# Moving a 3 MB weight load behind ten gathers, and three row sums to other places in VectorE's order, in a transformer tower on one core

## What is computed

```
def _L0_ffn_ref(x, ...):                            # mixture
    shared_out = swiglu(x, shared_gate, shared_up, shared_down)
    top_id = argmax(x @ gate_w.T); score = sigmoid(max(x @ gate_w.T))
    routed_out = sum over e of swiglu(where(top_id == e, x * score, 0), r_gate[e], r_up[e], r_down[e])
    return shared_out + routed_out

h = h + _L0_ffn_ref(_layernorm(h), ...)
h = h + _L1_attn_ref(_layernorm(h), ...)            # first: s = max(abs(x)) / 127 over the whole array, round(x / s)
h = h + _L1_ffn_ref(_layernorm(h), qweights, scales, ...)   # w = (q / 7.5 - 1) * scale
```

## Time and profile before

| what | value |
|---|---|
| median of 3 timed runs | 531.59 us (531.07 to 534.79) |
| profiled execution, its own time | 535.75 us |
| its span, first to last instruction | 533.9 us |
| PE busy | 413.0 us (77% of the span) |
| DVE busy | 313.8 us (59%) |
| ACT busy | 243.6 us (46%) |
| POOL busy | 154.4 us (29%) |
| mean granted TensorE clock | 0.862 of full speed |

### The profile page before, as it was taken

How to read it: one execution, slowest core, us unless ns; L and a number is a source line. 1 busy time by engine, 2 the same in 40 slices (tenths; PEclk the granted TensorE clock), 3 DMA queues, 4 the chain that set the end, 5 groups by cost and what they waited for, 6 DMA issues and landing times.

```text
span 533.9 us, 9523 instructions
## 1 busy us (share of the span) xinstructions
PE 413.0 (77%) x3502; PEld 305.2 (57%) x3503; DVE 313.8 (59%) x846; ACT 243.6 (46%) x519; POOL 154.4 (29%) x192
## 2 busy tenths in 40 slices
PE   5788864687999999999889976631894247699997
PEld 4556632565788866666546774210442135589996
DVE  2989877898364212223212137669898987636643
ACT  4345552566554112222122113792397568566651
POOL 3488762899120700000000063017010001213310
PEclk9999986699798999999999997565556556999999
DMA  8941113950033240111110081000000000000002
GB/s 275 401 176 21 21 24 70 425 234 2 1 132 136 92 126 26 54 41 41 39 41 29 26 319 30 1 1 2 2 0 0 1 6 1 1 0 2 1 20 75
DMA packets 19793, 38.64 MB, mean 72 GB/s; under 512 B 2136, under 2 KB 16164, under 8 KB 18340
## 3 DMA queue, kind: packets, MB, share of 16 engines
q1 hardware_dynamic: 18788, 35.41, 19.2%
q0 software_dynamic: 960, 2.62, 1.4%
HBM read 29.77 MB, written 7.01 MB: 69 GB/s over the span
## 4 chain that ended last, share of the span: by engine, by line
PE 56%; DVE 22%; ACT 11%; issue 6%; POOL 3%; DMA 1%; DVEq 0%; SPq 0%; ACTq 0%; POOLq 0%
PE psum L1331 11%; PE psum L1338 6%; PE psum L1363 6%; PE psum L2423 4%; PE psum L1377 4%; PE psum L2456 3%; PE psum L890 2%; PE psum L2462 2%; PE psum L1002 2%; PE psum L1355 1%; ACT experts L1739 1%; PE psum L2440 1%; DVE tile_peak L1767 1%; DVE front L1766 1%; PE psum L641 1%
## 5 line engine op out<-in xcount | busy, mean ns | idle before, releaser
L1331 PE MATMUL psum<-experts,ring 128*128 x136 | 64.3, 596 | 1.9 <-issue 1.2
L1155 DVE TENSOR_TENSOR ring<-ring,psum 128x512 f32<-128x512 f32 x17 | 11.7, 688 | 62.9 <-PE psum L1331 62.9
L1262 POOL DMA_INDIRECT front<-expert_results,slot_of x10 | 9.8, 981 | 125.0 <-DMA expert_results<-ring 122.2
L1338 PE MATMUL psum<-front,shared 128*128 128x256 f32 (+1 forms) x160 | 36.0, 380 | 0.0
L1331 PEld LDWEIGHTS psum<-experts,ring 128*128 128x128 f32 x136 | 23.3, 190 | 19.5 <-issue 19.4
L1338 PEld LDWEIGHTS psum<-front,shared 128*128 128x128 f32 x160 | 30.3, 197 | 3.5
L1363 PE MATMUL psum<-experts,ring 128*128 x136 | 32.1, 379 | 0.0
L1363 PEld LDWEIGHTS psum<-experts,ring 128*128 128x128 f32 x136 | 25.8, 190 | 10.3 <-issue 7.6
L2423 PE MATMUL psum<-experts 128*128 128x256 f32 (+1 forms) x120 | 27.5, 372 | 4.6 <-ACT experts L2486 4.6
L1461 ACT COPY ring<-psum 128x512 f32<-128x512 f32 x17 | 10.0, 586 | 42.4 <-PE psum L1355 42.4
L641 PE MATMUL psum<-experts,ring 128*128 128x256 f32 x108 | 25.1, 382 | 3.5 <-DVE experts L500 1.5
(11 more groups left out here) (364 smaller groups left out, 1081.5 us busy)
## 6 DMA issues: line engine op xcount, KB each, us to landing
experts<-in_experts SPq DMA_DIRECT2D x8, 1536.0 KB, 12.1
experts<-in_x SPq DMA_DIRECT2D x9, 384.0 KB, 8.4
expert_rows<-zeros SPq DMA_DIRECT2D x1, 2176.0 KB, 14.7
ring<-expert_rows SPq DMA_DIRECT2D x17, 128.0 KB, 2.1
shared<-in_shared SPq DMA_DIRECT2D x1, 1536.0 KB, 18.2
experts<-in_ffn_q SPq DMA_DIRECT2D x1, 1536.0 KB
experts<-in_ffn_s SPq DMA_DIRECT2D x1, 1536.0 KB
experts<-in_pos_embed SPq DMA_DIRECT2D x1, 1152.0 KB, 9.3
```

Of the source, the lines that this page charges most:

```text
L1155: nc.vector.tensor_tensor(o, o, up_bank(g), ALU.mult).then_inc(hidden_done.sem, 1)
L1331: mm = nc.tensor.matmul(bank, sl_xT[t % 2][:, k, :], slot_w(t, block, k, F), start=(k == 0), stop=(k == KD - 1))
L1338: mm = nc.tensor.matmul(o[:, b, 0:w], shared_w(block, k, (2 * half + b) * P, P), moe_x(c)[:, k, 0:w], start=(k == 0), stop=(k == KD - 1))
```

## The change

Two edits. On SyncE, the two 1.5 MB loads now wait until all ten gathers have landed. On VectorE, `row_sums(0)` stands ahead of `shared_added(3)` instead of behind it, and `row_sums(3)` stands behind the row shifts of pairs 0 and 1 instead of ahead of them. No instruction is added or taken away other than the five waits on SyncE.

```
                 if g == GROUPS:
                     row_sums(dve, step, 2)
-                    row_sums(dve, step, 3)
                     row_shift(dve, 0)
                     row_shift(dve, 1)
+                    row_sums(dve, step, 3)
+                if g == GROUPS - 2:
+                    row_sums(dve, step, 0)
                 if g >= 1 and shared_step(g - 1) is not None and shared_step(g - 1)[1] == 1:
                     shared_added(shared_step(g - 1)[0])
                 if g == GROUPS - 2:
-                    row_sums(dve, step, 0)
                     row_sums(dve, step, 1)
...
             sp.wait_ge(sl_down.sem, sl_down.done(SLOT_TILES - 1))
+            for c in range(NCH):
+                sp.wait_ge(rows_back[c], 32)
             sp.dma_start(ffn_q, ins["ffn_q"]).then_inc(l_ffn.sem, 16)
             sp.dma_start(ffn_s, ins["ffn_s"]).then_inc(l_ffn.sem, 16)
```

## The result

The changed kernel has a median of 531.00 us against 533.43 us for the kernel before (18 runs each). The ratio is 0.9959, with a 95% interval of 0.9940 to 0.9978: faster by 2.2 us, and by 1.2 to 3.2 within the interval. The forecast was a gain of 2.4 and a median of 529.2; the gain came, and the median stands 1.8 higher because the kernel before has 533.43 over these 18 runs and not the 531.59 of its first three.

A forecast was written before the change was run, and what follows sets the result against it. TensorE was taken as late through gathers slowed by the loads and VectorE's order. The mark's 327.75 - 325.35 = 2.4 us gain gave 531.59 - 2.4 = 529.2 us; range 526.8 to 532.8, the forecast's own 528.2 to 530.0.

The forecast's parts named there:

- the mark: Start of VectorE's fifth row sum, 327.75 in the profile before; its gain, 2.4 us, was taken as the kernel's.
- Step 1: VectorE: pair 0 lands at 312.15, so row sum 0 runs 312.20 to 314.15 in idle time, at no cost.
- Steps 2 to 4: `hidden(26)` starts at 317.65, TensorE's idle time falls from 3.81 to 0.7 us, row sum 2 runs 318.21 to 320.14.
- Step 5: VectorE ahead of the row shifts of pairs 0 and 1: 2.3 us of new idle time, waiting for POOL's `rstd`.
- Step 6: VectorE: row sum 3 from 322.55, then `shared_added(4)`, row sum 4 at 325.35 instead of 327.75: 2.4 us gained.
- POOL's start: First gather starts at 308.46, 2.5 us after the last store's issue; up to 0.8 us earlier without loads, taken as 0.
- Row sums under gathers: POOL's gather issues beside VectorE's row sums: no new cost taken; 0.3 us each would make the gain 1.8.
- The loads: They start at about 322.6 and land by 334; POOL's first use leaves 22 us of cover.
- (a): Gathers slow by themselves, the pair landing at 316.99 without the loads too: slower by 0.8 us, 532.4; 6%.
- (b): TensorE's clock in the projections: staying low, slower by 1.9 us, 533.5, 8%; up from the start, 527.4, 6%.
- (c): Something later is due at a fixed time, or the loads disturb instruction fetch: no gain, 531.6; 8%.
- (d): The change does not do what it says, TensorE still waiting for row sum 1; counted as (a).

The follow-up runs named there:

- third group: On a third chip: loads' wait alone 0.9933, new order alone 1.0009, changed kernel 0.9948, changed kernel with two `rstd` between eighth and ninth gather 0.9949.
- first group: On one chip: loads' wait alone 1.0004, new order alone 0.9986, changed kernel with row sum 3 ahead of row shifts 0.9995, with two `rstd` behind eighth gather 0.9944.
- the hold on POOL: Changed kernel with row sum 3 ahead of the row shifts, plus POOL waiting for `hidden(26)` ahead of its eighth gather: 0.9938 to the kernel before.

## Why the prediction was right, step by step

**The bound.** TensorE was late because VectorE was, and VectorE because the gathers shared the DMA engines with the loads. Shown: with the loads' wait alone the mark gains 3.0 us (21.8 to 18.8), with the order alone it loses 0.5. The prediction called the order on VectorE a second cause beside the landing. That was too much: with the gathers landing early, the order of before costs TensorE 2.44 us of idle time that nobody waits for. What row sum 0 ahead gains comes from VectorE, which does it in time that was idle (2.83 us in the loads' wait alone).

**Step 1.** Row sum 0 was put at 6.24 us behind the store; it began at 6.50, since the pair lands after 2.73 us and not 2.4. The addition of pair 3 hid the difference (0.57 us of idle time were left).

**Steps 2 to 4.** `hidden(26)` was put at 11.69 and measured at 11.72; TensorE's idle time at 0.7 and 0.71; the product at the upper clock at 3.45 and 3.87. The 3.45 was pair 3's product, read in the chain; the timeline gives that product 3.62 in both kernels. Nothing waited for the difference.

**Step 5.** The new wait for POOL was put at 2.3 us and measured at 2.04, in the place named. That it is a cost of the new order and not of the change as a whole is what the variants add: with row sum 3 ahead of the shifts it is gone, and the mark gains 1.2 to 1.6 us. The prediction saw that POOL takes some of the gain back, and left it open what that is worth.

**Step 6 and the sum.** The mark was put at 19.39 and measured at 19.20: a gain of 2.59 for 2.4, and the same 19.2 in both repetitions. The times are less steady than the mark: the changed kernel was 2.2, 1.0 and 2.8 us below before on its three occasions, so that the first came within 0.2 of the forecast is in part luck. The rest of the kernel from the mark on took 206.15 us before and 205.41 after, within the 204.5 to 206.2 that the traces with the signal on time show, so the 0.7 us that it adds in this pair of traces are not the change's.

**POOL's start.** The open 0.8 us between the store's landing and the first gather do not come from the loads: in every trace, with and without them, the first gather starts 2.47 to 2.50 behind the store. Taking 0 was right; the long end of the forecast's range had no ground.

**Row sums under gathers.** Ten gathers took 12.47 us from the first start to the last end (309.07 to 321.54), against 12.55 before (308.46 to 321.01), with three row sums beside them instead of two. The prediction took no new cost, and none came; but its reason, that the later row shows none, was a misreading. The cost is real and depends on which of the two begins first. The longest issue with a row sum beside it, from POOL's and VectorE's timelines of the loads' wait alone in the third group:

```profile
315.83 0.68 DVE L1628 TENSOR_TENSOR h<-h,front 128x512 f32<-128x512 f32 x1
315.87 1.46 POOL L1262 DMA_INDIRECT front<-expert_results,slot_of  x1 [0.30 <-issue]
```

In the 14 traces 24 issues begin while a row sum's addition runs, 0.04 to 0.54 us behind its start, and all of them end 1.49 to 1.52 us behind that start: 1.46 us long when they begin 0.04 behind it, 1.24 at 0.27 (317.26), 1.12 at 0.38 (316.63 here), 0.98 at 0.53 (319.31 here). Of the 36 that had begun before the row sum, 35 take 0.94 to 0.95, as the one at 318.81 did, 0.11 ahead of its row sum; the other stands behind an `rstd` and took 1.02, as it did in the trace in which it has no row sum beside it. So the most that one row sum cost is 0.5 us, and in sum it was 0.3 before and 0.2 here, by where they happened to fall. The rule of the Trainium skill, page "SBUF — State Buffer", section "Who interferes with whom", on two SBUF inputs against a GpSimd instruction that reads SBUF, agrees with the issues that begin inside a row sum, 1.46 us against 0.95; for those that had begun before it no trace here shows a cost.

**The loads.** They moved from 323 to 333 (84% at 326 GB/s), and L2325 at 356.45 is released by ScalarE. The cover was there.

**The rivals.** (a) needs slow gathers; with the loads in place it is what the order alone shows, +0.5 at the mark where 0.8 were worked out. (b) did not come: ScalarE's 18 evictions took 11.32 us, 11.42 before. (c) and (d) did not come in the changed kernel. A late signal, which no rival had, came on one chip with three of the variants: two of them (1.0004 and 0.9995) showed no gain there, and the third, with `rstd` among the gathers, kept its gain (0.9944). Whether the changed kernel does so wasn't tried. There is no trace of the kernel before on that chip either, but its median was 534.72 us there, and 531.78 to 532.37 on the three chips after it. In the four variants of that group the median lies 509.9 to 510.8 us above the mark. If that holds for the kernel before too, its mark was at 23.9 to 24.8 there (an estimate), some 2.6 us later than in its trace. Over all kernels with a trace the same difference is 509.6 to 512.0, which would still give 22.7. Then the ratios of all four follow from their marks of 24.4, 23.8, 25.1 and 21.8: the late signal would have hit the kernel before as well, and covered what the loads' wait gains. This is not shown.

## What to carry to other kernels

When a chain waits for small scattered transfers, look first at what big transfer was started just ahead of them, and where its data is used: here 3 MB had some 22 us of slack, and one wait on the queue that issues them gave all that the changed kernel gained, and by the mark 0.4 us more. Measure each part of a second edit alone, on top of the first: one part of the new order gained 0.8 to 1.2 us at the mark, the other cost 1.2 to 1.6. Ask of every instruction that waits what is queued behind it: the row shifts waited 2 us for POOL, and row sum 3 behind them could have run for about the second half of that.

## What the runs showed of the hardware

VectorE can go on up to 5 us after the end that the profile gives for the matmuls it waits for. In the first group it did so in three of four kernels (3.16, 5.23 and 3.12 us of idle time on VectorE with the releaser "remote"), and in the fourth VectorE was busy until later. In eight traces from three other chips the same place shows none. In the two kernels in which it went on latest, it did so (321.11 and 319.26) just after SyncE, which waits for the last gather, issued the load of `ffn_q` (320.99 and 319.08). In the third, two `rstd` instructions hold POOL between the eighth and the ninth gather. POOL's and VectorE's rows and the windows view there (last store at 302.54):

```profile
314.01 0.94 POOL L1263 DMA_INDIRECT front<-expert_results,slot_of  x1 [0.30 <-issue]
...
316.54 1.02 POOL L1263 DMA_INDIRECT front<-expert_results,slot_of  x1 [0.17 <-issue]
317.33 0.55 DVE L1160 TENSOR_TENSOR ring<-ring,psum 128x384 f32<-128x384 f32 x1 [3.12 <-remote]
316.50:317.50 1.00, 0.00 (x0) 0.00 (x0) 0.17 (x1) 0.00 (x0) 0.96 (x1) 1.00 0.00 0
```

VectorE went on at 317.33, 14.8 behind the store and 2 us earlier than in the other two, while the DMA engines moved nothing (0 GB/s). All this speaks for the gathers as the cause and shows nothing yet; the hold on POOL was meant to decide it, and came to a chip without the effect. It stays open.

An indirect DMA's issue on POOL that begins while VectorE adds two arrays from SBUF (128x512, 0.69 us) is held up, by up to 0.51 us (1.46 us long instead of 0.95); one that has begun before it is not (0.94 to 0.95).

Of TensorE's clock: in the changed kernel and with the loads' wait alone (third group) the last down product ran in 3.87 us after idle times of 0.71 and 2.44 us; with the order alone (third group) and before, it took 5.55 and 5.48 us after 4.28 and 3.81 us. In the four kernels of the first group it took 5.51, 6.87, 6.09 and 6.65 us after 3.79, 4.41, 5.82 and 5.89 us, so its length does not follow the idle time alone.
